# A decoder layer for 16 sequences: another order for the softmax shift, the queries and the self-attention of later batches

## The reference

```python
x = x + self_attention(layernorm(x))            # one head, 256 x 256
x = x + cross_attention(layernorm(x), context)  # 16 heads of 64; 1601 keys
x = x + ffn(layernorm(x))                       # a router picks 31 of the 256 rows; only they go through
                                                # a small 16-head attention and a 128-512-128 MLP
```

## Time and profile before

| | us |
|---|---|
| median of 3 executions | 2568.49 (2566.52 to 2568.88) |
| the profiled execution | 2568.49 |
| its span, first to last instruction | 2567.2 |

### The profile page before, as it was taken

One profiled execution on the slowest core, in us unless ns is written; L12 is line 12 of the kernel. 1 busy time (PEld: TensorE's weight loads), 2 busy tenths in 40 slices (PEclk: granted clock), 3 DMA queues, 4 the chain that ended last, 5 costly groups with the idle time before them and its releaser, 6 DMA issues. The chain is left out here.

```text
span 2567.2 us, 55548 instructions
## 1 busy us (share of the span) xinstructions
PE 2224.8 (87%) x22232; PEld 1627.5 (63%) x22232; DVE 2091.6 (81%) x3079; ACT 1690.2 (66%) x2835; POOL 1742.3 (68%) x980
## 2 busy tenths in 40 slices
PE   5898898988888889898988889888898988989984
PEld 3566665666666666665666666666665666667663
DVE  4888888888888878888888888888888888888973
ACT  2577676766766666676766667767676666767671
POOL 1477776776777666776777666766776766767782
PEclk8899999999999999998999999999999999999996
DMA  4000000000000000000000000000000000000000
GB/s 119 11 2 11 1 2 11 1 11 2 11 2 1 11 2 17 4 1 11 2 11 2 1 11 6 13 4 11 1 1 11 2 11 1 8 1 4 1 2 9
DMA packets 16959, 22.05 MB, mean 9 GB/s; under 512 B 5232, under 2 KB 14592, under 8 KB 16704
## 3 DMA queue, kind: packets, MB, share of 16 engines
q1 hardware_dynamic: 16704, 18.50, 2.3%
HBM read 16.27 MB, written 2.10 MB: 7 GB/s over the span
## 5 line engine op out<-in xcount | busy, mean ns | idle before, releaser
L1284 POOL TENSOR_TENSOR EL<-PF,EH 124x1024 f16<-124x1024 f32 x624 | 1497.4, 2414 | 304.4 <-ACT PF L736 220.8
L736 ACT ACTIVATE PF<-PS 124x512 f32<-124x512 f32 x1664 | 979.8, 596 | 505.6 <-PE PS L452 429.3
L906 DVE TENSOR_REDUCE pmax<-PS 128x1 f32<-128x806 f32 x1024 | 998.5, 989 | 254.2 <-PE PS L483 239.6
L466 PE MATMUL PS<-Ch,EH 123*128 123x97 f16 (+1 forms) x6656 | 798.9, 210 | 101.7 <-POOL EL L1284 70.7
L466 PEld LDWEIGHTS PS<-Ch,EH 123*128 123x128 f16 (+1 forms) x6656 | 621.8, 99 | 316.3 <-issue 142.5
L468 PE MATMUL PS<-Cl,EL 123*128 123x97 f16 (+1 forms) x6656 | 795.2, 210 | 0.0
L468 PEld LDWEIGHTS PS<-Cl,EL 123*128 123x128 f16 (+1 forms) x6656 | 611.9, 100 | 181.6 <-issue 17.4
L451 PE MATMUL PS<-AH,ChT 97*124 97x512 f16 x1664 | 660.8, 397 | 11.6 <-ACT PF L736 6.9
L452 PE MATMUL PS<-AL,ClT 96*124 96x512 f16 x1664 | 650.4, 391 | 0.0
L483 PE MATMUL PS<-ChT,AH 96*128 96x403 f16 x2048 | 547.4, 350 | 56.2 <-DVE AL L914 47.2
L892 DVE TENSOR_SCALAR EH<-PF 124x1024 f16<-124x1024 f32 x416 | 442.3, 1063 | 10.7 <-ACT PF L736 10.7
(11 more groups left out here) (209 smaller groups left out, 1576.9 us busy)
## 6 DMA issues: line engine op xcount, KB each, us to landing
Cf<-in_ctx SPq DMA_DIRECT2D x16, 599.6 KB
X<-in_x SPq DMA_DIRECT2D x16, 128.0 KB, 4.1
out_x<-X SPq DMA_DIRECT2D x16, 128.0 KB, 1.7
msk<-in_attention_mask SPq DMA_DIRECT2D x4, 256.0 KB, 4.5
AH<-mh SPq DMA_DIRECT2D x64, 2.0 KB
xWqT<-in_xWqT SPq DMA_DIRECT2D x2, 256.0 KB, 5.1
xWo<-in_xWo SPq DMA_DIRECT2D x2, 256.0 KB, 4.7
fw<-in_fw SPq DMA_DIRECT2D x2, 256.0 KB, 3.8
```

The lines of the kernel that those rows point to most:

```text
L466: pe.matmul(PS[:, 6, u0:u0 + DC + 1], EH[0:kr, r, qs], Ch[j][0:kr, t, :], start=(t == 0 and q == 0), stop=False, skip_group_check=True)
L736: act.activation(PF[:, n % PRING, :], PS[0:KP, 4 + n % 2, :], ACT.Exp).then_inc(sg("ex"), 1)
L906: dve.tensor_reduce(pmax[:, b % 2, ht, half:half + 1], PS[:, 2 * half:2 * half + 2, 0:NKEY], AX_XY, ALU.max).then_inc(sg("max_rd"), 1)
L1284: pool.tensor_tensor(EL[:, r - 1:r + 1, :], PF[:, f - 1:f + 1, :], EH[:, r - 1:r + 1, :], ALU.subtract).then_inc(sg("lo_pool"), 1)
```

## The change

Only the order of the list is changed; every engine's code for a step is as it was, and so is the number of steps. `PLACES` has 28 tiles of a batch: 14, 16, 18, 20, 27, 29, 31, 33, 40, 42, 44, 46, 53, 55, 57, 59, 66, 68, 70, 72, 79, 81, 83, 85, 92, 94, 96 and 98.

- **Chunks.** All 64 chunks of batch b+1 now stand within batch b: none in tiles 0 to 18, 8 in tiles 19 to 26, none in tiles 27 to 32, 56 in tiles 33 to 96, none after. One `redmax` (tile 98) and one `placemax` (tile 100) serve all 16 heads, where there were four of each.
- **Queries** of b+1: tiles 18, 20, 33, 46, 59, 66, 70, 72. **Transposes** of the context: 14, 16, 27, 29 (before: 31, 42, 55, 57).
- **Self-attention**: that of batch b+2, in tiles 34 to 68.
- **Batch 0** has 48 chunks of its own and all 64 of batch 1, 112 in all (before: 71), 14 `q` (before: 8) and the self-attention of batch 2; batch 15 has no chunk, no `q` and no self-attention.
- **The start**, ahead of the first `st`: two `q` (before: three), the scaling and splitting of context 1, and the self-attention of batch 1 and the `trig` step between the first 16 chunks.
- **The `c_...` steps** stand at tiles 79, 81, 83, 85, 92, 94, 96, 98 (before: 59, 68, 72, 81, 83, 85, 94, 98) of the same batches.

```diff
-SA_PLACES = (5, 7, 16, 20, 29, 33, 46)
-TURN_PLACES = (31, 42, 55, 57)
-CHOSEN_PLACES = (59, 68, 72, 81, 83, 85, 94, 98)
-Q_LEAD, MAX_LEAD, ROW_LEAD = 38, 36, 8
+PLACES = [k for k in range(AV_LAG + 6, TILES) if (k - AV_LAG) % KT in (6, 8, 10, 12)]
+LAST = TILES - 4
@@ beside_plan
-        places = iter([TILES * b + k for b in range(4 * gq + 4, 4 * gq + 8) for k in CHOSEN_PLACES])
+        places = iter([TILES * b + k for b in range(4 * gq + 4, 4 * gq + 8) for k in PLACES[20:28]])
@@
-def ahead(n):
-    todo = [(KT * hp - Q_LEAD, ("q", n, hp)) for hp in range(HP)]
-    for h in range(0, H, EARLY):
-        first = KT * h // 2
-        c = chunks(n, h, h + EARLY)
...
-            todo += spread(c, first - MAX_LEAD, first - ROW_LEAD - 3)
-        todo += [(first - ROW_LEAD - 2, ("redmax", n, h, h + EARLY)), (first - ROW_LEAD, ("placemax", n, h, h + EARLY))]
@@ plan
+    if n < B and b >= 1:
         todo += [(AV_LAG + 1 + x, ("ctx_hi", n, x)) for x in range(2)]
         todo += [(AV_LAG + 4 + x, ("ctx_lo", n, x)) for x in range(2)]
-        todo += list(zip(TURN_PLACES, transposes_of(n)))
-        q = SA_PLACES
-        todo += list(zip((0, 3, *q[:6], q[5] + 2, q[5] + 5, q[6]), self_attention(n)))
+        todo += list(zip((p[0], p[1], p[4], p[5]), transposes_of(n)))
+        todo += list(zip((p[2], p[3], p[7], p[11], p[15], p[16], p[18], p[19]), queries_of(n, 0, HP)))
+        c = chunks(n, 0, H)
+        todo += spread(c[:8], p[2] + 1, p[4] - 1) + spread(c[8:], p[6] + 2, LAST - 4)
+        sa_places = (p[8], p[9], p[10], p[12], p[13], p[14], p[17])
+    if b == 0:
+        todo += list(zip((0, 2, 4, 6, 8, 10), queries_of(0, 2, HP)))
+        for q in range(1, 4):
...
+            todo += [(end, ("redmax", 0, h, h + EARLY)), (end + 1, ("placemax", 0, h, h + EARLY))]
...
+        todo += spread(chunks(1, 0, H), p[12] + 2, LAST - 3)
+        sa_places = (p[15], p[16], p[17], p[18], p[19], p[20], p[23])
+    if n < B:
+        todo += [(LAST - 2, ("redmax", n, 0, H)), (LAST, ("placemax", n, 0, H))]
+    if b + 2 < B:
+        q = sa_places
+        tiles = (q[0] - 6, q[0] - 3, *q[:6], q[5] + 2, q[5] + 5, q[6])
+        todo += list(zip(tiles, self_attention(b + 2)))
@@ whole_order
-    out += [step for _, step in sorted(ahead(0), key=lambda x: x[0]) if _ < 0]
+    out += queries_of(0, 0, 2) + [("ctx_max", 1), ("sigma", 1), ("ctx_scale", 1)] + context_of(1)
+    beside = self_attention(1) + [("trig",)]
+    for k, step in enumerate(chunks(0, 0, EARLY)):
+        out.append(step)
+        if k < len(beside):
+            out.append(beside[k])
+    out += [("redmax", 0, 0, EARLY), ("placemax", 0, 0, EARLY)]
```

## The result

The changed kernel takes 2705.06 us (four executions, 2703.5 to 2706.83), the kernel before 2567.51 beside it: 1.0537 times, 95% interval 1.052 to 1.0555. It is slower by 137.5 us. The forecast was slower by 53 (2621, range 2545 to 2700): the sign was right, the size not, and the time lies just outside the range.

A forecast was written before the change was run, and what follows sets the result against it. The bound was taken as shared: PE's chain where DVE has slack, DVE where it has none. Start 92, batch 0 174, 13 x 152, groups 64.8, batches 142 and 105.5, end 65.9, plus 1.3 outside the span: 2621, range 2545 to 2700.

The forecast's parts named there:

- The start: Before the first tile: added query, context and self-attention work delays the first exponential by 18, to 92 instead of 73.8.
- Batch 0: Its 41 more chunks at DVE's full price and six queries give 174 against 148.6, DVE 0.91 busy.
- Batches 14 and 15: Last batches: 142 without self-attention; 105.5 without chunks or queries, four times two quiet windows plus 3 for selection.
- The middle batch: Batches 1 to 13: 152 each against 149.9, chosen between 153.4 by PE's sum and 149.8 by DVE's.
- The 32 open tiles: Tiles without chunks in a middle batch: 31.5 from batch 15's windows plus 3.0 for context copies, 34.5.
- The quiet crowded tiles by PE's chain: Thirteen crowded tiles without extras: PE's chain wants 16.6, DVE 16.1; under 16.5 in tiles 70 to 96 would refute.
- The slack that let small extras pass is gone, so I charge 1.1 each: 16.5: Crowded tiles of a middle batch: 15 us of extra DVE work, charged at 1.1 per us.
- 34.5, 98.9, 2 and 1.5: Middle-batch terms: tiles without chunks; 72 others by PE with turn_u/proj and chunks; uneven DVE operations; first chunk's wait behind its query.
- The single `placemax`: Ahead of the next batch: no new wait, over 5 us ahead; 1 to 2 per batch if DVE were late.
- The groups' steps: The `c_...` steps, two tiles apart among denser chunks: 2 more per group, +6 to 64.8, range -5 to +12.
- every lump costs a run-up: Rival, 13%: extras at 1.4 per us, 5 for uneven operations, 10 per group; batch 161, total about 2760.
- The crowded tiles run DVE nearly full: Rival, 12%: PE and DVE overlap better, DVE 0.905 busy in crowded tiles; batch 143.7, total 2513, faster.

The follow-up runs named there:

- run 1: Kernel before with only batch b+2's self-attention moved to tiles 34 to 68 of batch b (batch 2's in batch 0, tiles 49 to 84): 2690.62 us, ratio 1.0475.
- run 2: Changed kernel with the self-attention of batches 3 to 15 put back to tiles 0 to 38, sa_f staying at 68: 2655.05 us, ratio 1.0343.
- run 5: Changed kernel with its queries spread to tiles 18, 20, 33, 46, 56, 64, 74, 83: 2754.61 us, ratio 1.0733.
- run 8: Kernel before with batch b+2's self-attention moved to quiet tiles 58 to 94 of batch b: 2545.4 us, ratio 0.9919.
- run 14: Changed kernel with its queries at tiles 18, 31, 33, 46, 59, 65, 71, 81: 2676.16 us, ratio 1.042.
- run 3: Changed kernel with each chunk's DVE reduction over half the scores, PE's work the same: 2580.99 us, ratio 1.0057.
- run 4: Kernel before with each chunk's DVE reduction over half the scores: 2433.53 us, ratio 0.9479.
- run 6: Changed kernel with the selection's row and rank at tiles 30 and 31 instead of 36 and 37: 2686.71 us, ratio 1.047.
- run 9: Kernel before with no chunks in tiles 0 to 18 and 27 to 32 from batch 1 on, and four queries moved: 2626.65 us, ratio 1.0222.
- run 10: Kernel before with 8 chunks instead of 64 from batch 2's on: 2309.07 us, ratio 0.899.
- run 11: Changed kernel with 8 chunks instead of 64 from batch 2's on: 2443.93 us, ratio 0.9513.

## Why the prediction had the sign and missed the size

Of the 84 us between forecast and result, some 63 are in batches 1 to 13, 16 in batches 14 and 15, and 4 in batch 0; 2 are the profiled execution's distance from the median, and the start took 1 less.

**The start** held: 91.0 for the forecast 92. **The end** too: 65.8 for 65.9.

**Batch 0** was 178.2 for 174, DVE busy 0.89 of it, for 0.91. That is slightly low; to reckon dense chunks at DVE's full price was right.

**Batches 14 and 15** came out 147.5 and 116.0 for 142 and 105.5; together 16 us of the miss. Batch 14 was put 10 below a middle batch and is 9.7 below one (157.2), so its 5.5 are the middle batch's miss again. For batch 15 I multiplied the two quietest windows by four. They are the same after (11.96, 13.77), but the windows of the router's selection, tiles 26 to 51, without any chunk, are these:

```profile
2547.77:2563.48 15.71, 11.75 (x137) 7.62 (x134) 12.60 (x19) 10.61 (x18) 13.59 (x8) 1.00 0.01 2
2563.48:2582.37 18.89, 14.84 (x153) 10.74 (x150) 9.27 (x25) 12.70 (x20) 15.89 (x8) 0.91 0.00 1
```

They take 34.60 for 25.6: 9 for batch 14's selection, where I had allowed 3.

**The middle batch**, 13 times in the sum, is where it failed: 157.5 (mean of the plain ones 157.7) for 152.

- *The 32 open tiles* (34.5) were near enough: 13.12 for the first 13, with context work, where the term makes 14.0.
- *The quiet crowded tiles by PE's chain* (16.6 for 13, 1.7 more with a `turn_u`) were even too dear: 15.90 for tiles 78 to 90. (Tiles 91 to 103, 16.35, hold only five chunks.) The falsifier "under 16.5 without self-attention" is met. Crowding chunks as such into quiet tiles costs less than I said.
- ***"The slack that let small extras pass is gone, so I charge 1.1 each: 16.5"*** is the step that failed. It prices a step by its volume on DVE alone. With the other terms as they stand (34.5, 98.9, 2 and 1.5), a batch of 157.5 leaves 20.6 for these extras, 1.4 per us; the other 1.4 of the miss is the choice of 152 where PE's sum gave 153.4. The price is not even: in tiles 52 to 77 the batch takes 45.55; the quiet windows give 15.90 and 17.6 for the same tiles, so 12.0 is for extras which add 1.17 + 3.41 = 4.6 of DVE work: 2.6 per us. The same extras bring PE matmuls, which the charge left out: PE is busy 38.5 us in these tiles, and some 31 by the quiet window. What runs 1, 2, 5, 8 and 14 show in its place is that the price depends on the place: the same self-attention costs +123 in all or -22 by its tiles, the same eight queries +50 or -29 against the change. With DVE relieved of half its reductions (runs 3 and 4) the distance between the two orders stays, at 147.

Where PE's time goes can be summed over batches 1 to 13. Per batch, the change is 7.4 longer: PE's idle time grew by 6.8 (18.2 to 25.0), its busy time by 0.6. The idle time ahead of chunks whose reduction is late grew by 10.1 and that ahead of `av` by 3.2; chunks' waits for `AL` fell by 2.0 and the waits ahead of the shared bank's steps by 5.2. In the change the late reductions are thus the wait that grew, and hand-overs on the shared bank the one that shrank; run 6 shows that the first is not lost time in full.

The change's 7.8 per plain batch was taken apart by one edit at a time: crowding, with four queries moved, +3.7 (run 9), self-attention's place 3.2 (run 2), the queries' places 1.9 (run 14). That makes 8.8. They are not independent parts: moving self-attention cost 7.0 in the even order (run 1) and 3.2 in the crowded one. And few chunks leave 8.9 (runs 10, 11). So each of the three is shown to cost time, their shares only by these pairs; by which wait each does so is argued.

- *The single `placemax`* is no new wait, as said. PE's `st` waits for the transfer into `AH` once in the whole run:

```profile
PE PS L458 <- DMA AH<-mh: 2.2, 1, 2.2
```

- *The groups' steps* (+6, range -5 to +12) hardly changed: against the four batches without any, the eight that carry them (4, 5, 6, 8, 9, 10, 12, 13) have an excess of 57 before and 58 after.

Of the rivals, "every lump costs a run-up" (161 per batch, 2760) was nearer in mechanism: a lump on DVE with both pairs of banks full stops PE, 6.59 behind the selection. The prediction saw this lump already at work in the kernel before, and there misread it: the wait of 2.33 behind the selection was a query's for the shared bank (L493 for `junk`), not for a pair of banks. The rival's 1.4 per us of extras is what the batch shows; too high were its 5 for uneven operations and its 10 per group. "The crowded tiles run DVE nearly full" had its share of truth in tiles 78 to 90, where DVE is busy 15.70 of 15.90, yet no whole batch did.

What stays open is the exact split between hand-overs on the shared bank, reductions that come late, DVE operations that POOL holds up (below), PE's own matmuls among crowded chunks, and PE's lower clock: in tiles 39 to 51 it was granted 0.82, with the 6.59 us pause, for 0.87 before. No run moves one of these alone.

## What to carry to other kernels

Price a step that is moved by its work on every engine and by what stands next to it in every in-order queue and on every shared buffer, not by its busy time on one engine. Keep steps that share one PSUM bank off each other's tiles, and fill the quiet stretches rather than clear others; here putting self-attention into the quiet tiles of the old order gave the only gain (2543 to 2545). Where the sum goes by busy times, cut the busiest engine's work in half in both versions: if their distance stays, it is not the amount of that work that separates them, though it may still be when it is done. And take a wait that has grown for a loss only when the stretch around it has grown as much.

## What the hardware showed that I had not expected

DVE was busy 2214.7 us in the change and 2091.6 before, with 45 instructions fewer (one `redmax` for four). Most of the excess, 107.5 us, is in two operations that read and write SBUF, while POOL works too. By the profile's groups, after the change:

```profile
L899 DVE TENSOR_SCALAR EH<-PF 124x1024 f16<-124x1024 f32 x416 | 513.4, 1234 | 53.2 <-ACT PF L743 53.2
L908 DVE TENSOR_TENSOR EL<-PF,EH 124x1024 f16<-124x1024 f32 x208 | 304.9, 1466 | 1.8 <-ACT EH L750 1.7
```

`EH` took 1063 ns on the mean before, `EL` 1291. The shortest `EH` is 0.66, the longest 2.67. The three long operations shown from 477.42 on can be read against POOL's timeline of the same stretch:

```profile
476.67 2.12 POOL L1291 TENSOR_TENSOR EL<-PF,EH 124x1024 f16<-124x1024 f32 x1
478.75 1.27 POOL L1299 TENSOR_TENSOR Un<-U,rden_u 128x384 f32<-128x384 f32 x1
479.98 5.18 POOL L1291 TENSOR_TENSOR EL<-PF,EH 124x1024 f16<-124x1024 f32 x2
```

POOL's first `EL` ends at 478.79, and DVE's `EH` ends 0.55 later. POOL's `Un` ends at 480.02, and DVE's `EL` 1.08 later. POOL's pair of `EL` ends at 485.16, and `rank`, an operation of 128x2 that took 0.16 at 432.25 in the kernel before, where POOL stood idle, ends at 485.18 after 1.62. Each of them ends only when, or shortly after, the instruction that POOL was running does. The Trainium skill ("SBUF — State Buffer", section Terms, on the shared port pair) says that DVE and GpSimd take this pair as an exclusive lock for a whole instruction and that the loser blocks; these rows agree. It is a rule that spoke against packing DVE and that the prediction left out. The reductions, which read PSUM, are 987 ns in the mean, as before (989). How much of the loss it makes is not shown: DVE's busy time grew by 9.9 in batch 2 and by 5.7 in that of run 9, and no run changes POOL's work.
